# Second attention in a fused two-layer kernel: transposed scores by a second product with the maxima subtracted in it

## The reference

```python
x = x + _L0_xattn_ref(_layernorm(x), ctx_1024, ...)      # first attention
x = x + _L0_ffn_ref(_layernorm(x), L0_ffn_rhs)           # quantised linear layer
x = x + _L1_xattn_ref(_layernorm(x), ctx_1024, w_q, w_k, w_v, w_o)   # second attention
x = x + _L1_ffn_ref(_layernorm(x), gate_w, ...)          # routed and shared experts

def _L1_xattn_ref(query, kv_source, w_q, w_k, w_v, w_o):  # 16 heads of 32, 120 keys for each of 8 batches
    q = (query @ w_q.T).reshape(B, T_q, N_HEADS, HEAD_DIM)
    k = (kv_source @ w_k.T).reshape(B, T_kv, N_HEADS, HEAD_DIM)
    v = (kv_source @ w_v.T).reshape(B, T_kv, N_HEADS, HEAD_DIM)
    attn = softmax(einsum('bqhd,bkhd->bhqk', q, k) * HEAD_DIM ** -0.5)
    out = einsum('bhqk,bkhd->bqhd', attn, v).reshape(B, T_q, D_MODEL)
    return out @ w_o.T
```

## Time and profile before

| | |
|---|---|
| median of the runs | 1243.36 us (1242.11 to 1245.54) |
| profiled execution | 1246.73 us, span 1245.0 us |
| PE busy | 1189.6 us, 96% of the span |
| DVE busy | 950.4 us, 76% |
| ACT busy | 709.2 us, 57% |
| POOL busy | 595.6 us, 48% |
| second attention, products from `scores` of tile 0 to `product` of tile 31 | about 232 to 602 us |

### The profile page before, as it was taken

The page is one execution under the profiler, slowest core; times in us unless marked ns, Lnnn a source line. Parts: engine busy times, 40 slices in busy tenths (PEclk is TensorE's granted clock), DMA queues, the critical chain, the costliest instruction groups (busy, mean ns, idle before and its releaser), DMA issues.

```text
span 1245.0 us, 29420 instructions
## 1 busy us (share of the span) xinstructions
PE 1189.6 (96%) x10692; PEld 823.2 (66%) x10692; DVE 950.4 (76%) x2005; ACT 709.2 (57%) x1988; POOL 595.6 (48%) x685
## 2 busy tenths in 40 slices
PE   6888998799999999999899999999999999999996
PEld 3555665578888888887444444777777777666663
DVE  5889898889999999988577787677777785645450
ACT  3377778799989999897354322222222231465652
POOL 0037668736777666733300025365555320176745
PEclk9999999999999999999999999999999999999999
DMA  9612024133544545553781060312221531599987
GB/s 346 216 40 97 1 27 52 44 94 125 166 148 156 182 138 160 171 179 110 187 190 22 1 169 2 103 22 82 36 69 35 181 109 35 147 257 232 270 132 97
DMA packets 157567, 150.28 MB, mean 121 GB/s; under 512 B 78544, under 2 KB 111472, under 8 KB 157424
## 3 DMA queue, kind: packets, MB, share of 16 engines
q1 hardware_dynamic: 139584, 125.94, 35.0%
q0 software_dynamic: 13248, 21.15, 9.0%
q10 hardware_dynamic: 4592, 1.32, 0.5%
HBM read 84.93 MB, written 57.19 MB: 114 GB/s over the span
## 4 chain that ended last, share of the span: by engine, by line
PE 83%; DVE 7%; ACT 3%; issue 3%; DMA 2%; POOL 1%; ACTq 0%; SPq 0%; DVEq 0%; POOLq 0%
PE bank L121 29%; PE bank L2132 15%; PE bank L2125 13%; PE bank L1503 6%; PE bank L955 4%; PE bank L1435 4%; PE bank L1456 3%; PE bank L1450 2%; PE bank L1421 2%; ACT att_land L1353 2%; PE bank L1024 1%; PE bank L872 1%; DMA q_rows<-att_land 1%; PE bank L891 1%; DVE front_amax L768 1%
## 5 line engine op out<-in xcount | busy, mean ns | idle before, releaser
L1630 POOL DMA_INDIRECT lists<-att_land x128 | 134.8, 1053 | 229.6 <-DVE att_land L1770 115.3
L1353 ACT ACTIVATE att_land<-bank,att_land 128x120 f32<-128x120 f32 x512 | 178.3, 376 | 10.8 <-DVE att_land L1221 10.6
L2125 PE MATMUL bank<-att_land 128*128 128x512 f16 x768 | 176.2, 379 | 0.6 <-DVE program_logits L1304 0.6
L1952 ACT ACTIVATE att_land<-program_x 128x512 f32<-128x512 f32 x40 | 25.2, 631 | 195.1 <-DVE program_x L2094 195.1
L121 PE MATMUL bank<-program_xs,program_wgu 128*128 128x512 f16 x576 | 128.7, 379 | 0.6 <-DVE att_land L1730 0.6
L2125 PEld LDWEIGHTS bank<-att_land 128*128 128x128 f16 x768 | 75.0, 98 | 82.1 <-issue 0.6
L1353 ACT ACTIVATION_READ_ACCUMULATOR att_land<-bank,att_land 128x1 f32 x512 | 113.4, 222 | 0.0
L121 PE MATMUL bank<-att_land 128*128 128x128 f16 (+1 forms) x1560 | 101.2, 222 | 0.5 <-DVE att_land L1278 0.5
L121 PEld LDWEIGHTS bank<-program_xs,program_wgu 128*128 128x128 f16 x576 | 56.3, 98 | 67.5 <-DVE att_land L1730 1.1
L1221 DVE TENSOR_REDUCE att_land<-bank 128x4 f32<-128x480 f32 x128 | 82.3, 643 | 21.0 <-PE bank L1421 20.5
L121 PEld LDWEIGHTS bank<-att_land 128*128 128x128 f16 x1560 | 91.2, 98 | 3.7 <-DVE att_land L1278 0.7
(11 more groups left out here) (304 smaller groups left out, 2836.2 us busy)
## 6 DMA issues: line engine op xcount, KB each, us to landing
att_land<-q_rows SPq DMA_DIRECT2D x96, 128.0 KB, 2.7
xn_rows<-att_land SPq DMA_DIRECT2D x37, 256.0 KB, 3.1
out_rows<-att_land SPq DMA_DIRECT2D x37, 256.0 KB, 6.5
q_rows<-att_land SPq DMA_DIRECT2D x32, 256.0 KB, 3.0
xt_tiles<-att_land SPq DMA_DIRECT2D x32, 256.0 KB, 2.1
x_rows<-program_x SPq DMA_DIRECT2D x8, 1024.0 KB, 4.6
att_land<-x_rows SPq DMA_DIRECT2D x8, 1024.0 KB, 5.4
program_xs<-xt_tiles SPq DMA_DIRECT2D x28, 256.0 KB, 4.8
```

The source lines that it names most:

```text
L1353: last = act.activation(prob[:, c, h, :], ps_s[c % 2][:, h, :], ACT.Exp, bias=nmax[:, u % 2, c, h:h + 1], accum_out=rsum[:, u % 2, n:n + 1])
L1630: pool.indirect_dma_start(out=io["lists"], out_offset=bass.IndirectOffsetOnAxis(ap=index[:, t, k:k + 1], axis=0), in_=load[:, t, k, :], in ...
L2125: last = pe.matmul(ps_y[i][:, :], hid[:, c % 2, a, i * P:(i + 1) * P], wd[:, q, c, :], start=c == 0 and n == 0, stop=c == NC - 1 and n == 2)
```

## The change

The transposed exponentials are no longer made by transposing the exponentials. PE makes the scores twice: once with queries as rows, for the maxima only (one PSUM bank instead of two), and once with keys as rows (`shifted_scores`). For the second product the keys get a 97th row of the constant 64 and the queries a 97th row that holds the negated maxima divided by 64. That row comes from `max_transposed` (PE), a copy `maxima` on ACT and a transfer. ACT then takes the exponential of 120 x 512 twice: to f16 (the high half) and to f32 in SBUF (`expf`); DVE subtracts the one from the other (`prob_low`, now from SBUF). Values get two columns of ones behind each head (34 columns), so the sums of the rows come out of `outputs`; `inverse_sums` and `weighted` work on two halves of eight heads. Queries have three buffers instead of two. The rows' normalisation (`rows`, `gate_rows`) goes from GpSimd to ACT, the weights' split from GpSimd to ACT (high) and DVE (low). The orders of all engines' steps are new, with one more step of lag; `JOIN` and `TAIL` change in four entries.

```diff
 def attention1(g, io, m, banks, f):
-    LEAD, LAG = 6, 5
-    PLACE = (1, 0, 2, 3)
+    LEAD, LAG = 6, 6
...
-    ps_sf, ps_p = (banks[1], banks[2]), chunked[3:5]
+    ps_s = banks[1][:, 0:HC * J].rearrange("p (h j) -> p h j", h=HC)
+    ps_m = banks[1][0:HEADS, 0:P]
+    ps_t = chunked[2:4]
...
     def sync(sp):
         def step(t):
+            w = t - 1
+            if live(w):
+                sp.wait_ge(s["m_ok"], w + 1)
+                need(sp, c4["t_mm"], KC * (w - 2))
+                row = g.queries[w % 3][KD:KD + 1].rearrange("q r (c i) -> q (r c) i", c=KC)
+                sp.dma_start(row, mrow[0:HEADS, w % 2]).then_inc(m_in[w % 2], 16)
...
+            if live(v):
+                sp.wait_ge(s["g_lo"], v + 1)
+                sp.dma_start(io["xt_tiles"][v, :, :], gT[:, v % 2].rearrange("p q k n -> p (q k n)")).then_inc(gt_out[v % 2], 16)
             if live(t) and t % TB == 3:
                 b = t // TB
                 if b + 1 < B:
-                    need(sp, c4["s_mm"], KC * TB * b)
+                    need(sp, c4["t_mm"], KC * TB * b)
...
     def vector(dve):
-            dve.tensor_reduce(nmax[:, u % 2, c], ps_s[c % 2][:, :, :], AX.X, ALU.max, negate=True).then_inc(c4["max"], 1)
+            need(dve, s["m_mm"], u - 1)
+            dve.tensor_reduce(nmax[:, u % 2, :, c], ps_s[:, :, :], AX.X, ALU.max, negate=True).then_inc(c4["max"], 1)
...
+        def prob_low(u, c):
+            if not live(u):
+                return
+            dve.wait_ge(c4["exp"], KC * u + c + 1)
+            dve.tensor_tensor(pT[0:J, c, 1], expf[0:J, c % 2], pT[0:J, c, 0], ALU.subtract).then_inc(c4["p_lo"], 1)
+
         def step(t):
...
+            prob_low(t - 2, 1)
+            inverse_sums(t - 3, 1)
+            query_low(t + 1)
+            weighted(t - 3, 1)
+            rows_low(t + 2)
+            maximum(t, 0)
+            prob_low(t - 2, 2)
+            output_low(t - 3)
+            yield
+            maximum(t, 1)
+            prob_low(t - 2, 3)
+            residual(t - 4)
+            gate_stats(t - 4)
+            inverse_sums(t - 2, 0)
+            aggregate(ln, t + 5)
+            weighted(t - 2, 0)
+            aggregate(lg, t - 4)
+            maximum(t, 2)
             prob_low(t - 1, 0)
...
+            gate_low(t - 5)
             stats(ln, t + 6)
             first_rows(t + 3)
...
+            maximum(t, 3)
+            logits(t - 6)
+            if 3 < t <= 3 * B + 1 and t % 3 == 1:
+                b = t // 3 - 1
+                dve.wait_ge(w_hi, b + 1)
+                dve.scalar_tensor_tensor(g.wgu[:, b, 1, :], raw[:, :], WS, g.wgu[:, b, 0, :], ALU.mult,
+                                         ALU.subtract).then_inc(w_lo, 1)
...
     def scalar(act):
+            act.activation(pT[0:J, c, 0], ps_t[c % 2][0:J], ACT.Exp)
+            act.activation(expf[0:J, c % 2], ps_t[c % 2][0:J], ACT.Exp).then_inc(c4["exp"], 1)
+
+        def maxima(u):
+            if live(u):
+                act.wait_ge(s["m_mm"], u + 1)
+                need(act, m_in[u % 2], 16 * (u // 2))
+                act.activation(mrow[0:HEADS, u % 2], ps_m, ACT.Copy, scale=1 / WS).then_inc(s["m_ok"], 1)
...
         def step(t):
-            prob_high(t - 1, 0)
+            maxima(t - 1)
             query_high(t + 1)
+            exponentials(t - 2, 2)
             rows_high(t + 2)
+            exponentials(t - 2, 3)
+            output_high(t - 3)
+            gate_rows(t - 5)
             yield
...
+            exponentials(t - 1, 0)
+            rows(t + 4)
...
+            exponentials(t - 1, 1)
+            gate_high(t - 5)
...
     def tensor(pe):
+            need(pe, c4["max"], KC * u + c)
+            for h in range(HC):
+                last = pe.matmul(ps_s[:, h, :], g.queries[u % 3][0:KD, h, c * P:(c + 1) * P],
+                                 g.keys[0:KD, b % 2, h, c * J:(c + 1) * J], start=True, stop=True)
+            last.then_inc(c4["s_mm"], 1)
+
+        def max_transposed(u):
+            if live(u):
+                pe.wait_ge(c4["max"], KC * u + KC)
+                pe.transpose(ps_m, nmax[:, u % 2].rearrange("p r c -> p (r c)"), g.ident[:, :]).then_inc(s["m_mm"], 1)
...
+                last = pe.matmul(ps_t[c % 2][0:J, h, :], g.keys[0:KD + 1, b % 2, h, c * J:(c + 1) * J],
+                                 g.queries[u % 3][0:KD + 1, h, c * P:(c + 1) * P], start=True, stop=True)
+            last.then_inc(c4["t_mm"], 1)
...
         def step(t):
+            shifted_scores(t - 2, 2)
+            rows_transposed(t + 2)
             outputs(t - 2, 0)
+            scores(t, 0)
+            product(t - 4, 0)
+            shifted_scores(t - 2, 3)
+            outputs(t - 2, 1)
+            scores(t, 1)
+            output_transposed(t - 3)
+            product(t - 4, 1)
+            yield
+            shifted_scores(t - 1, 0)
             outputs(t - 2, 2)
...
+            scores(t, 2)
+            queries(t + 2, 0)
+            gate_transposed(t - 5)
+            shifted_scores(t - 1, 1)
             outputs(t - 2, 3)
...
+            scores(t, 3)
+            gate_logits(t - 6)
             queries(t + 2, 1)
+            max_transposed(t)
```

More of the change, by code:

```diff
@@ L139, in packed_queries @@
 def packed_queries(sp, g, io, u, done):
-    spread(sp, g.queries[:, u % 2], io["q_rows"][u], (0, 0, 1), done[u % 2])
+    spread(sp, g.queries[u % 3], io["q_rows"][u], (0, 0, 1), done[u % 3])
 class Norm:
@@ L156, in __init__ @@
         self.rstd = m.sb(name + "_rstd", [P, 4, 1])
[L157 to L173, removed]
+        self.shift = m.sb(name + "_shift", [P, 4, 1])
+        self.stats, self.aggr, self.root, self.ok = (m.sem(f"{name}_{n}") for n in ("stats", "aggr", "root", "ok"))
     def inverse_root(self, pool, g, u, d):
@@ L1090, in attention1 @@
     qT = g.early(4 * D, [P, 2, KC, P], f16)
[L1091 to L1095, removed]
+    oT = g.early(5 * D, [P, 2, 2, KC, P], f16)
+    expf = g.early(7 * D, [P, 2, HC, P])
+    nmax = g.early(SM, [P, 2, HC, KC])
+    rinv = g.early(SM + 2 * HEADS, [P, 2, HH])
+    gwf = g.early(SM + 3 * HEADS, [P, KC, E + 1])
@@ L1111, in attention1 @@
[L1111 to L1116, removed]
+    ps_y = banks[6]
+    s = {n: m.sem("b_" + n) for n in ("xt_mm", "xt_hi", "xt_lo", "q_mm", "q_hi", "q_lo", "m_mm", "m_ok", "inv", "o_tr", "o_hi",
+                                      "o_lo", "y_mm", "x_new", "g_tr", "g_hi", "g_lo", "l_mm", "l_ok")}
@@ new lines, in scores, with shifted_scores @@
+            for h in range(HC):
[3 more added lines that the diff above has]
+        def max_transposed(u):
+            if live(u):
+                pe.wait_ge(c4["max"], KC * u + KC)
+                pe.transpose(ps_m, nmax[:, u % 2].rearrange("p r c -> p (r c)"), g.ident[:, :]).then_inc(s["m_mm"], 1)
+        def shifted_scores(u, c):
+            if not live(u):
+                return
+            b = u // TB
+            if c == 0:
+                pe.wait_ge(m_in[u % 2], 16 * (u // 2 + 1))
+            if u == 0 and c == 0:
+                pe.wait_ge(f.a["sim"], NT)
+                pe.wait_ge(f.one_ok, 2)
+            if u == 0 and c == 1:
+                pe.wait_ge(f.a["p_lo"], NT)
+            if u == TB and c == 0:
+                pe.wait_ge(f.one_ok, 3)
@@ L1441, in outputs @@
                 return
[L1442 to L1445 removed]
+            half = c // 2
+            if c % 2 == 0:
+                need(pe, of_ok[half], u)
+            if u == 0 and c == 0:
+                pe.wait_ge(f.one_ok, 2)
+                pe.wait_ge(f.a["y_ok"], NT)
+            if u == 0 and c == 2:
+                pe.wait_ge(f.q["t_ok"], NT)
             pe.wait_ge(c4["p_lo"], KC * u + c + 1)
             for h in range(HC):
[L1448 to L1451 removed]
+                n = c * HC + h
+                out = ps_o[half][:, n % HH]
+                hi, lo = g.v1h[0:J, u // TB, n], g.v1l[0:J, u // TB, n * DH:(n + 1) * DH]
+                pe.matmul(out, pT[0:J, c, 0, h, :], hi, start=True, stop=False)
+                pe.matmul(out[:, 0:DH], pT[0:J, c, 0, h, :], lo, start=False, stop=False)
+                last = pe.matmul(out, pT[0:J, c, 1, h, :], hi, start=False, stop=True)
             last.then_inc(c4["o_mm"], 1)
@@ L1484, in output_transposed @@
             if live(u):
-                pe.wait_ge(s["of"], u + 1)
+                for half in range(2):
+                    pe.wait_ge(of_ok[half], u + 1)
                 need(pe, s["o_lo"], u)
-                need(pe, s["xt_lo"], min(u + 5, NT))
-                need(pe, s["l_ok"], u - 2)
+                need(pe, s["xt_lo"], min(u + 6, NT))
+                need(pe, s["l_ok"], u - 3)
                 transposed(ps_x, of).then_inc(s["o_tr"], 1)
```

327 lines of the change are left out of this document (130 added, 197 removed).

## The result

The changed kernel takes 1329.44 us, the median of four runs (1325.77 to 1331.81). The kernel before, run beside it, takes 1244.45 (1242.11 to 1247.85). The ratio is 1.068, 95% interval 1.064 to 1.071: slower by 85 us. The forecast was 1306, with a range from 1278 to 1330. The profiled execution after took 1329.32 us, with a span of 1327.6.

What follows compares the result with a forecast made beforehand. PE was taken to bound the kernel before, at 10.71 us a step; the change adds a 12.55 us path of waits. Terms 36.5 + 4.7 + 2.0 + 4 + 2.5 + 5 + 8.4 = 63.1 on 1243.4 give 1306 us, range 1278 to 1330.

Steps and rivals of the forecast that it cites:

- every link that was named: Attention step: path of waits through PE, ACT and DVE from one `max_transposed` to the next, 12.55 us in all.
- DVE's two waits for ACT's copies: Each attention step: DVE waits about 1 us ahead of `output_low` and about 0.5 ahead of `gate_low`.
- The faster rival: Attention steps: engines slip, only totals count, a step is 10.3 to 10.7 us; time 1222 to 1240, say 1234; chance 0.06.
- 21 full steps: Steps 5 to 25, with all links there: 12.55 us each against 10.81 before, 36.5 us in all.
- four steps without `stats`: From step 26 `stats` has no tile left: four steps of 11.98 us, 4.7 us in all.
- weights' splits: Steps where DVE splits weights: about 0.25 of its 1.2 us reaches the path, eight times, 2.0 us.
- start: While the first attention still runs, scores wait for maxima behind that stage's work: 5 us, between 0 and 12.
- keys: Next four tiles' keys are loaded later in SP's step: 1.2 us at each of seven changes, 8.4 us.
- row of maxima: New 4 KB transfer before `shifted_scores`, with 4.9 us of cover: costed at zero, at most 21 us.
- the last steps: End of attention: 4 us for steps 30 and 31, 2.5 us for one more step of lag.
- the third rival: Slower still: the maxima's row comes late or PE's clock falls in the gaps; 1320 to 1390 us, chance 0.11.
- the prediction's signs of being wrong: Mid-attention: a pace under 11 us, PE without gaps, or PE waiting for the row of maxima's transfer.

Runs made afterwards that it cites:

- The last kernel: Reordered kernel with two groups' low halves on GpSimd; weights' low split moved to GpSimd over two steps, SP issues tokens a step later: 1241.1 us, ratio 0.996.

## Why the prediction was right

**The mechanism was.** The list above has every link that was named, in the named order, and DVE's two waits for ACT's copies are 0.97 and 0.38 us (about 1 and 0.5 named). A full step was put at 12.55 us and took 12.61. That the path sets it is shown by both kinds of run: work taken from the path shortens the step by about its links (11.54, 12.14) or down to the next bound (10.71), work taken from beside it changes nothing (12.61 with less on ACT, 12.61 with less on DVE).

**Totals were nearly right too, as bounds behind the path.** DVE was put at 10.3 for a step without a split and at 10.7 on the mean of three steps, one of them with a split. With the path shortened the step is 10.71 and 10.58, in the second with DVE busy for 96% of it (10.15 of 10.57), and it falls to 10.18 when DVE is relieved; a step with a split takes 11.7, which makes 10.96 on the mean of three. PE was put at 9.96: with nothing else in the way its step is 10.17, 98.7% of it busy (105.59 of 107), so 10.04. The faster rival thus described the kernel that the change could have been (1241.1 us, near its 1234), not the one that it was.

**Prices.** The low half was kept at one price for SBUF and PSUM, against a row of a table (the Trainium skill, "VectorE: DVE Perf Modes", "The TRN2 errata") that has a smaller fixed part from SBUF. In the changed kernel 32 of them from SBUF take 681 ns on the mean, 40 from PSUM in the same stretch before took 677: the trace disagrees with that row here. The exponential was taken like a copy, 0.49 apart; it is 0.47 to 0.50.

**The sizes of some terms were not.** Adding the excess of the profile's steps over 10.81 gives the 82.6 us again, beside the sum of 63.1:

| term | predicted | measured | from |
|---|---|---|---|
| 21 full steps | 36.5 | 37.8 | 21 x (12.61 - 10.81) |
| four steps without `stats` | 4.7 | 4.8 | 51.74 - 4 x 10.81, less keys, tokens and a split |
| weights' splits | 2.0 | 1.1 | eight of 0.07 to 0.16 |
| start | 5 | 7.3 | step 4 begins at 296.6, before at 289.3 |
| keys | 8.4 | 12.9 | six changes, 1.01 to 3.06 each; the seventh is in the start |
| row of maxima | 0 | 2.7 | steps 12 and 24, 1.09 and 1.57 |
| tokens issued by ACT | not seen | 1.8 | step 26, 13.82 for 12.02 |
| the last steps | 6.5 | 14.2 | 82.6 less the rest |

The cost of a change of keys goes with the clock. Each is the step's length less that of the same step with early keys. In the stretches from 494.80 and 387.80 the granted clock is 1.00, and a change costs 1.01 and 1.76 us, where 1.2 was predicted (its own figures, 4.9 less 3.8, give 1.1). In the other three of five full steps it falls to 0.89 (as from 441.20), and a change costs 2.55 to 3.06. PE's list at two of them, and in the last steps:

```profile
444.75 0.56 PE L1437 MATMUL bank<-att_land 96*128 96x120 f16 x4 [2.31 <-DMA att_land<-k_rows]
445.10 2.34 PE L1539 MATMUL bank<-att_land 128*128 128x512 f16 x5
...
497.81 0.37 PE L1437 MATMUL bank<-att_land 96*128 96x120 f16 x4 [1.73 <-DMA att_land<-k_rows]
498.02 1.46 PE L1539 MATMUL bank<-att_land 128*128 128x512 f16 x6
...
639.86 2.55 PE L1539 MATMUL bank<-att_land 128*128 128x512 f16 x6
```

Six products of 512 take 1.46 us at the full clock; at 639.86 the same six take 2.55. So the third rival, PE's clock falling in the gaps and a late row of maxima, was true in places, and the time lies in its range of 1320 to 1390 too. What parts it from the forecast is the ordinary step, whose clock is 1.00 and which waits for no row. That the clock would hold there was not well founded: the prediction called a step with PE busy for 79% nearer to the stretch at 1.00 than to the one at 0.83, but its rows have PE busy for 76% at 1.00 and for 81% at 0.83, and 79% is nearer to the 81%.

The clock is part of the end's excess as well: the stretch from 640 has a granted clock of 0.73. The last kernel, with the detours gone, still takes 60.8 us from the start of its step 29 to the shared expert's line (granted clock 0.97), where the changed kernel takes 66.2 (0.92) and the kernel before, by its 10.81 a step, 51.9. So some 9 of the 14.2 us are not the path's. How much of them is the clock, and how much the one more step of lag, which the changed kernel and the last one share, no run separates; it stays open.

The row of maxima stayed inside its bound of 21 us. It came late where weights and `x_rows` fall into one step ahead of it: in steps 12 and 24 it landed 6.4 and 6.9 us after it was asked for, elsewhere after 1.6 to 5.1, and 4.9 had been given as its cover. PE waiting for that row was one of the prediction's signs of being wrong; it shows in these two steps alone.

So the forecast of 1306 was 23 us under the median: 19.5 are in the table, nearly all from start, keys, row, tokens and end, the terms for single steps and not the term for every step, and 3.4 come from the profiled run before, which was that much over its median. That 1329.44 still lies in a range that ends at 1330 is in good part luck: that end stood for links 5% longer and dearer keys, while the links came out 0.5% longer (12.61 for 12.55) and the tokens and most of the end's excess had no place in it.

## What to carry to other kernels

Where engines run lists in order, add up the totals, and then follow one whole step along its semaphores and list orders until it closes on itself: the longest such path sets the pace, and a move that shortens an engine's list wins nothing off it. What stands ahead of a reduction that another engine waits for is on the path, so the low halves and statistics that nobody waits for go behind it. Look where an engine idles before a piece that is late: the same split of weights cost up to 3.4 us a step in one piece of GpSimd's list and nothing there in two pieces, a step apart.

## What the runs showed of the hardware

A short wait of PE can cost more than itself: after 2.31 us of waiting for keys the next products ran slower and the step's granted clock was 0.89, while after 2.26 us at another change of keys the clock stayed at 1.00; the runs don't say what parts the two. The length of the wait does not: in the kernel without group 0's second exponential a wait of 1.92 us for keys was followed by a step at 0.89, in the one without group 1's a wait of 1.92 by a step at 1.00. A 4 KB transfer asked for right behind 1.5 MB on the same queue (539.15) let PE go only at 547.43.
